# A fused network of attention, experts and gated taps: the sum of 16 weighted rows moves to GpSimd and TensorE, constants load in order of need, and each engine gets a new order

## What is computed

```python
x = _layernorm(x + _L0_attn_ref(x, ...))   # 16 heads of 8, softmax(q k' / sqrt(8) - slope * |i - j|) v, projection
x = _layernorm(x + _L0_ffn_ref(x, ...))    # top 2 of 8 experts silu(x W1 + b1) * (x W3 + b3) W2 + b2, and a shared one
x = _layernorm(x + _L1_attn_ref(x, ...))   # the block that the change touches, below
x = _layernorm(x + _L1_ffn_ref(x, ...))    # top 2 of 8 linear experts

# _L1_attn_ref, offsets 2^j * tau, of which 16 distinct ones are under 256
attn = softmax(stack([sum(q * shift(k, off)) * scale for off in OFFSETS]) + pos_bias)
out = sum(attn[off] * shift(v, off) for off in OFFSETS if off < N)
return (out * sigmoid(x @ w_gate + b_gate)) @ w_out + b_out
```

## Time and profile before

| | |
|---|---|
| runs | 1625.95 us median of 3 (1625.87 to 1630.54) |
| profiled execution | 1623.99 us, span 1622.2 us |
| busy share of the span | PE 87%, PEld 67%, DVE 84%, ACT 56%, POOL 46% |
| chain that ended last | DVE 39%, PE 39%, issue 10%, ACT 6%, DMA 2%, POOL 2%, SP 1% |
| TensorE clock granted, mean | 0.969 of 2.4 GHz |
| DMA | mean 111 GB/s |

### The profile page before, as it was taken

The page is one execution under the profiler, slowest core; times in us unless marked ns, Lnnn a source line. Parts: engine busy times, 40 slices in busy tenths (PEclk is TensorE's granted clock), DMA queues, the critical chain, the costliest instruction groups (busy, mean ns, idle before and its releaser), DMA issues.

```text
span 1622.2 us, 34112 instructions
## 1 busy us (share of the span) xinstructions
...
## 2 busy tenths in 40 slices
...
GB/s 170 91 86 131 121 107 101 128 134 123 95 127 134 100 101 128 135 124 92 128 132 102 101 127 133 105 107 134 113 102 114 134 122 88 119 92 87 77 45 39
DMA packets 83560, 179.69 MB, mean 111 GB/s; under 512 B 9771, under 2 KB 65835, under 8 KB 66219
## 3 DMA queue, kind: packets, MB, share of 16 engines
...
## 4 chain that ended last, share of the span: by engine, by line
DVE 39%; PE 39%; issue 10%; ACT 6%; DMA 2%; POOL 2%; SPq 1%; DVEq 0%; ACTq 0%; POOLq 0%
PE bPV L518 8%; DVE mneg L998 7%; DVE nDy L938 5%; PE bTU L547 4%; PE b L556 4%; DVE wb L900 4%; PE bTU L548 4%; DVE wb L961 3%; DVE gc L862 3%; ACT x L727 3%; PE bS L535 3%; PE b L421 2%; PE bTU L465 2%; DVE gat L979 2%; PE bTU L480 2%
## 5 line engine op out<-in xcount | busy, mean ns | idle before, releaser
L998 DVE TENSOR_REDUCE mneg<-bS 128x2 bf16<-128x512 f32 x512 | 342.2, 685 | 68.1 <-PE bS L538 68.1
L1058 POOL TENSOR_TENSOR wb<-wb 128x1024 f32<-128x1024 f32 x64 | 150.4, 2350 | 524.2 <-DVE wb L900 524.2
L1066 POOL TENSOR_TENSOR prod<-kC,qC 128x512 f32<-128x512 f32 x256 | 367.4, 1470 | 17.5 <-ACT kC L658 17.3
L696 ACT ACTIVATE sil<-bTU,b 128x256 f32<-128x256 f32 x288 | 133.2, 474 | 327.4 <-PE bTU L548 227.7
L686 ACT ACTIVATE P<-bTU 128x512 f32<-128x512 f32 x512 | 280.3, 597 | 32.9 <-PE bTU L482 32.3
L1078 POOL TENSOR_TENSOR h<-ub,gBcb 128x256 f32<-128x256 f32 x256 | 182.8, 727 | 248.9 <-DVE ub L1011 214.5
L535 PE MATMUL bS<-stack 96*128 96x256 bf16 x1024 | 225.7, 279 | 32.0 <-DVE mneg L998 25.8
L480 PE MATMUL bTU<-stack 97*128 97x256 bf16 x1024 | 214.0, 277 | 17.3 <-ACT P L686 15.3
L538 PE MATMUL bS<-dist,identh 128*128 128x128 f16 x1024 | 200.7, 223 | 0.0
L482 PE MATMUL bTU<-dist,identh 128*128 128x128 f16 x1024 | 194.2, 221 | 0.0
L547 PE MATMUL bTU<-x1T,w 128*128 128x256 f32 x576 | 181.0, 396 | 2.0 <-DVE ub L1011 2.0
...
## 6 DMA issues: line engine op xcount, KB each, us to landing
...
```

The costliest lines, as they stand in the source:

```text
L998: v.tensor_reduce(mneg[:, :, k], bS[k % 2][:].rearrange("p (a b) -> p a b", a=TT), op=ALU.max, axis=AX.X, negate=True).then_inc(dveS.done( ...
L1066: tt_(prod[:, 2 * p:2 * p + 2, :], shifted(kC, p), qC[:].unsqueeze(1).to_broadcast([128, 2, T]), ALU.mult).then_inc(poolC1.done("prod", p), 1)
```

## The change

- The first of VectorE's three additions becomes a third addition on GpSimd (`C2.add.2`, rows 0 to 3 plus rows 8 to 11), in its queue behind `C1.prod.1`.
- TensorE sums the remaining four rows with the identity as weights, four accumulating matmuls of 128x128 by 256 columns (`C2.sm`), into one of the three banks that are used in turn.
- `C2.gt` reads that bank instead of a row in SBUF. VectorE's three additions are gone.
- SyncE first loads only what pass 0 needs (xT and six DMAs, `ld_first`), then the score tables; the other 19 constant DMAs come behind `A1.rows.2` of pass 0. TensorE waits for them at the start of pass 1, and VectorE and ScalarE make the small tables (`tables()`) at the end of pass 1.
- All five queues get a new order.

```diff
 ORDER = {
     "pe": """
-        B2.z A1.qk S.s.0 A1.v A2.ST.0 A2.ST.1 S.s.1 S.s.2 A2.ST.2 A2.ST.3 A2.ST.4 S.s.3 S.s.4 A2.ST.5 A2.ST.6
-        A2.PV.0 B.xT A2.ST.7 S.s.5 D.xT A2.ST.8 B.lg C1.xT D.lg S.s.6 A2.ST.9 A2.ST.10 A2.PV.1 A2.ST.11 C1.qk
-        A2.ST.12 A2.ST.13 S.s.7 S.s.8 A2.ST.14 A2.ST.15 D.y.0 C1.vg B.cT A2.PV.2 S.s.9 D.y.1 B.ab.0 A2.PV.3 B.ab.1
-        S.s.10 B.ab.2 S.s.11 D.y.2 A3.pT S.s.12 B.ab.3 B.ab.4 S.s.13 C2.out B.ab.5 S.s.14 C1.sc A3.aT C1.scT B.ab.6
-        B.ab.7 B.ab.8 S.s.15 B.z C1.wT A3.out D.y.3 M.mT""",
+        A1.qk S.s.0 S.s.1 B2.z A2.ST.0 A1.v S.s.2 A2.ST.1 A2.ST.2 S.s.3 A2.ST.3 A2.ST.4 A2.ST.5 S.s.4 A2.ST.6
+        A2.PV.0 B.xT A2.ST.7 S.s.5 C1.xT S.s.6 D.xT A2.ST.8 A2.ST.9 B.lg S.s.7 D.lg A2.ST.10 A2.ST.11 A2.PV.1
+        A2.ST.12 A2.ST.13 C1.qk S.s.8 A2.ST.14 A2.ST.15 S.s.9 C1.vg D.y.0 A2.PV.2 D.y.1 B.cT B.ab.0 S.s.10 B.ab.1
+        S.s.11 S.s.12 A2.PV.3 S.s.13 C2.sm B.ab.2 A3.pT S.s.14 B.ab.3 B.ab.4 C2.out B.ab.5 S.s.15 C1.sc A3.aT B.ab.6
+        C1.scT B.ab.7 B.z D.y.2 D.y.3 A3.out C1.wT B.ab.8 M.mT""",
     "act": """
-        A1.qk A2.exp.0 A2.exp.1 A2.exp.2 A2.exp.3 C2n.nm A2.exp.4 A3n.nm A2.exp.5 B.xT D.xT B2.nm A2.exp.6 A2.exp.7
-        A2.exp.8 A2.exp.9 C1.xT D2.nm A2.exp.10 A2.exp.11 G.ge A2.exp.12 C1.qk A2.exp.13 A2.exp.14 B.cT A2.exp.15
-        B.ab.0 B.ab.1 A3.cp B.ab.2 B.ab.3 C1.vg B.ab.4 B.ab.5 C1.sc B.ab.6 A3.aT C1.exp B.ab.7 B.ab.8 C1.wT M.mT""",
+        A1.qk A2.exp.0 A2.exp.1 A2.exp.2 A2.exp.3 A2.exp.4 C2n.nm A3n.nm B2.nm A2.exp.5 A2.exp.6 B.xT C1.xT D.xT
+        D2.nm A2.exp.7 A2.exp.8 A2.exp.9 A2.exp.10 A2.exp.11 A2.exp.12 G.ge C1.qk A2.exp.13 A2.exp.14 A2.exp.15 B.cT
+        B.ab.0 B.ab.1 A3.cp C1.vg B.ab.2 B.ab.3 B.ab.4 C1.sc B.ab.5 A3.aT B.ab.6 C1.exp B.ab.7 C1.wT B.ab.8 M.mT""",
     "dve": """
-        B2.res D2.mom N.root.0 S.max.0 A1.rest N.root.1 S.max.1 S.max.2 N.root.2 A1.v N.root.3 S.max.3 A1.mid A1.lo
-        C2.pv.0 C2.pv.1 C2.pv.2 C2.pv.3 S.max.4 S.max.5 S.max.6 G.rank C2.pv.4 C2.pv.5 C2.pv.6 C2.pv.7 G.weigh
-        S.max.7 S.max.8 C2.add.0 D.acc.0 C2.add.1 D.acc.1 S.max.9 B.wu.0 B.wu.1 C2.add.2 S.max.10 C2.gt B.wu.2
-        D.acc.2 S.max.11 A3.rec S.max.12 C2.res A3.num S.max.13 B.wu.3 B.wu.4 B.wu.5 C1.mx S.max.14 S.max.15 B.wu.6
-        C1.sum B.wu.7 B.wu.8 A3.res D.acc.3""",
+        S.max.0 S.max.1 A1.rest B2.res D2.mom A1.v N.root.0 S.max.2 N.root.1 N.root.2 A1.mid N.root.3 S.max.3
+        S.max.4 A1.lo C2.pv.0 C2.pv.1 C2.pv.2 C2.pv.3 S.max.5 S.max.6 S.max.7 G.rank C2.pv.4 C2.pv.5 C2.pv.6 C2.pv.7
+        G.weigh D.acc.0 S.max.8 D.acc.1 S.max.9 S.max.10 S.max.11 B.wu.0 B.wu.1 S.max.12 C2.gt B.wu.2 S.max.13
+        A3.rec A3.num S.max.14 C2.res B.wu.3 S.max.15 B.wu.4 C1.mx B.wu.5 B.wu.6 C1.sum B.wu.7 A3.res D.acc.2 B.wu.8
+        D.acc.3""",
     "pool": """
-        C2.add.0 C2.add.1 C1.prod.0 C1.prod.1 C1.prod.2 C1.prod.3 C1.prod.4 C1.prod.5 C1.prod.6 C1.prod.7 B.h.1
-        B.h.2 B.h.3 B.h.4 B.h.5 A3.xbo B.h.6 B.h.7 C2.xb B.h.8""",
+        C2.add.0 C2.add.1 C1.prod.0 C1.prod.1 C2.add.2 C1.prod.2 C1.prod.3 C1.prod.4 C1.prod.5 C1.prod.6 C1.prod.7
+        B.h.1 B.h.2 B.h.3 B.h.4 A3.xbo B.h.5 B.h.6 C2.xb B.h.7 B.h.8""",
     "sp": """
-        C2.wb A1.part.0 A1.part.1 X.xT A3.x A1.part.2 B.cT A1.rows.0 B.cb A1.rows.1 A1.rows.2 D2.out C1.dw M.m C1.wb""",
+        C2.wb D2.out A1.part.0 A3.x A1.part.1 A1.part.2 B.cT X.xT B.cb A1.rows.0 A1.rows.1 A1.rows.2 C1.dw M.m C1.wb""",
 }
...
-        turn = [(what[-2:], n) for what, n in ORDER["pe"] if what in ("A2.ST", "B.ab", "D.y")]
+        turn = [(what[-2:], n) for what, n in ORDER["pe"] if what in ("A2.ST", "B.ab", "D.y", "C2.sm")]
...
-        consts = [(wqk0, "wqk0"), (bqk0, "bqk0"), (qs0, "qs0"), (wv0, "wv0"), (wo0, "wo0"), (gw0, "gw0"), (gw1, "gw1"),
+        first_consts = [(wqk0, "wqk0"), (bqk0, "bqk0"), (qs0, "qs0"), (wv0, "wv0")]
+        consts = [(wo0, "wo0"), (gw0, "gw0"), (gw1, "gw1"),
                   (b1, "b1"), (b3, "b3"), (b2, "b2"), (wc, "wc"), (bc, "bc"), (woc, "woc"), (ident, "ident"),
                   (hsum, "hsum"), (least, "least"), (posd, "posd"), (oobd, "oobd")]
         score_consts = [(identh, "identh"), (dist, "dist")]
         expert_consts = [(w13, "w13"), (w2, "w2"), (ew, "ew")]
...
-        N_CONST, N_SCORE, N_EXPERT = len(consts) + 1 + 3 * TT, len(score_consts) + 9, len(expert_consts)
+        N_CONST, N_SCORE, N_EXPERT = len(consts) + 1 + 2 * TT, len(score_consts) + 9, len(expert_consts)
+
+        N_FIRST = len(first_consts) + TT
...
-            for dst, name in consts:
-                sp.dma_start(dst[:], A[name]).then_inc(ld_const, 16)
-            sp.dma_start(identb[:].bitcast(U16), A["identb"]).then_inc(ld_const, 16)
+            for dst, name in first_consts:
+                sp.dma_start(dst[:], A[name]).then_inc(ld_first, 16)
             for tt in range(TT):
-                for dst, name in ((bv0, "bv0"), (bo0, "bo0"), (boc, "boc")):
-                    sp.dma_start(dst[:, tt, :], bass.AP(A[name].tensor, 0, [[0, 128], [1, 128]])).then_inc(ld_const, 16)
+                sp.dma_start(bv0[:, tt, :], bass.AP(A["bv0"].tensor, 0, [[0, 128], [1, 128]])).then_inc(ld_first, 16)
...
+                    if t == 0 and (what, n) == ("A1.rows", 2):
+                        for dst, name in consts:
+                            sp.dma_start(dst[:], A[name]).then_inc(ld_const, 16)
+                        sp.dma_start(identb[:].bitcast(U16), A["identb"]).then_inc(ld_const, 16)
+                        for tt in range(TT):
+                            for dst, name in ((bo0, "bo0"), (boc, "boc")):
+                                sp.dma_start(dst[:, tt, :],
+                                             bass.AP(A[name].tensor, 0, [[0, 128], [1, 128]])).then_inc(ld_const, 16)
...
-            pe.wait_ge(ld_const, 16 * N_CONST)
-            pe.wait_ge(setup_dve, SETUP_DVE)
-            pe.wait_ge(setup_act, SETUP_ACT)
+            pe.wait_ge(ld_first, 16 * N_FIRST)
...
+                if t == 1:
+                    pe.wait_ge(ld_const, 16 * N_CONST)
+                    pe.wait_ge(setup_dve, 12)
+                if t == LAG["C1"]:
+                    pe.wait_ge(setup_dve, SETUP_DVE)
+                    pe.wait_ge(setup_act, SETUP_ACT)
...
+                    if what == "C2.sm" and (e := r["C2"]) is not None:
+                        take(turn_bank("sm", 0), ("C2", dveC2, "gt", 0), t)
+                        o = bTU[turn_bank("sm", 0)]
+                        pe.wait_ge(poolSum.sem, poolSum.count(e, "add", 2))
+                        for x in range(4):
+                            i = mm(o[:, 0:T], ident[:], pv[:, x, :], start=(x == 0), stop=(x == 3))
+                        i.then_inc(peC2.done("sm"), 1)
...
+            act.wait_ge(setup_act, 1)
+
+            def tables():
+
+                act.wait_ge(ld_const, 16 * N_CONST)
+                nc.scalar.mul(bc[:, 0:1], bc[:, 0:1], q_scale).then_inc(setup_act, 1)
...
+                act.wait_ge(setup_dve, SETUP_DVE)
...
+            dve.wait_ge(ld_first, 16 * N_FIRST)
+            dve.wait_ge(setup_dve, 12)
+
+            def tables():
+
+                dve.wait_ge(ld_const, 16 * N_CONST)
...
-                    if what == "C2.add" and n == 0 and (e := r["C2"]) is not None:
-
-                        dve.wait_ge(poolC2.sem, poolC2.count(e, "add", 1))
-                        v.tensor_tensor(pv[:, 0:4, :], pv[:, 0:4, :], pv[:, 8:12, :], ALU.add).then_inc(dveC2.done("add", 0), 1)
...
-                    if what == "C2.add" and n == 1 and (e := r["C2"]) is not None:
-                        dve.wait_ge(dveC2.sem, dveC2.count(e, "add", 0))
-                        v.tensor_tensor(pv[:, 0:2, :], pv[:, 0:2, :], pv[:, 2:4, :], ALU.add).then_inc(dveC2.done("add", 1), 1)
...
-                    if what == "C2.add" and n == 2 and (e := r["C2"]) is not None:
-                        dve.wait_ge(dveC2.sem, dveC2.count(e, "add", 1))
-                        v.tensor_tensor(pv[:, 0, :], pv[:, 0, :], pv[:, 1, :], ALU.add).then_inc(dveC2.done("add", 2), 1)
                     if what == "C2.gt" and (e := r["C2"]) is not None:
 
-                        dve.wait_ge(dveC2.sem, dveC2.count(e, "add", 2))
+                        dve.wait_ge(peC2.sem, peC2.count(e, "sm"))
                         dve.wait_ge(actC1.sem, actC1.count(e, "g"))
                         dve.wait_ge(peC2.sem, peC2.count(e - 1, "out"))
-                        v.scalar_tensor_tensor(gat[:], tg[:], 1.0, pv[:, 0, :], ALU.add,
+                        v.scalar_tensor_tensor(gat[:], tg[:], 1.0, bTU[turn_bank("sm", 0)][:, 0:T], ALU.add,
                                                ALU.mult).then_inc(dveC2.done("gt"), 1)
...
 
-                        pool.wait_ge(dveC2.sem, dveC2.count(e, "pv", 4 * n + 3))
-                        tt_(pv[:, 8 * n:8 * n + 4, :], pv[:, 8 * n:8 * n + 4, :], pv[:, 8 * n + 4:8 * n + 8, :],
-                            ALU.add).then_inc(poolC2.done("add", n), 1)
+                        if n < 2:
```

(10 more changed lines are left out.)

60 lines of the change are left out of this document (30 added, 30 removed).

## The result

The changed kernel takes 1618.42 us, median of 5 runs (1615.07 to 1621.27), against 1625.95 for the kernel before; the ratio is 0.9938, with a 95% interval of 0.9914 to 0.9961. It is faster by 0.6%, where 1635 and "slower" were forecast; the range, 1606 to 1655, holds it. The profiled execution took 1620.27 us, its span 1618.5, 3.7 less than the span before.

A forecast was written before the change was run, and what follows sets the result against it. No engine is full; a dependence loop of three legs closing once per pass bounds the kernel. Profiled 1624.0 + 5 (steady passes) + 6 (last passes) - 1.5 (start) = 1633.5, plus 2.0 for the median: 1635; range 1606 to 1655.

The forecast's parts named there:

- Leg A: Stretch from the end of `C2.pv.7` to the start of `C1.sc`: GpSimd's queue would bound it, 16.3 us against 15.85.
- lower bound, 15.9: Bound on Leg A, if a second copy of an addition started behind a product loses no more than 1.9 us.
- TensorE's 15.2: When TensorE would be through its Leg A queue, in us after `pv.7`, 1.1 us before GpSimd's last product.
- the first rival: GpSimd is faster than its rows, so TensorE would end Leg A: pass 45.4 us, about 1606 in all; chance 0.15.
- Leg B: Stretch from the start of `C1.sc` to the start of `A3.res`, TensorE's: 9.9 us, taken as 10.0, against 10.60.
- Leg C: VectorE's stretch from the start of `A3.res` to the end of `pv.7`: 20.2 us, bounds 20.0 to 20.6, against 19.89.
- `G.rank` did not wait for `D.lg`: Sign in Leg C: `D.lg` returns at about 16.1 us, `G.rank` wants it at 16.3; a wait would refute the forecast.
- before `B.wu.3`, for the whole GpSimd queue: Expected sign: VectorE idle before `B.wu.3`, which needs `B.h.1` and hence all of GpSimd's queue.
- The pass: Steady pass, the sum of its three legs: 46.5 us against 46.3, bounds 45.8 to 47.2; +5 us over 25 full passes.
- The start: New loading order of constants: first matmul at about 7 us, `S.s.0` of pass 1 at 33.2; -1.5 us (-4 to +1).
- The last passes: Passes t = 32 to 36: additions among GpSimd's products and cold matmuls cost about +6 us (+2 to +9).
- rival 3: TensorE's clock falls more often because of longer idle around `A2.PV.0`: 8 more passes make 26 us, 1661; chance 0.2.

The follow-up runs named there:

- before_no_adds: The kernel before without VectorE's three additions and nothing in their place, so the gate reads an incomplete sum: 1607.62 us, ratio 0.9869.
- dummy_two: The changed kernel with an extra VectorE addition of 128x960, two SBUF inputs, on scratch ahead of `C2.gt`: 1616.56 us, one execution.
- dummy_one: The changed kernel with an extra VectorE maximum over 128x960, one SBUF input, ahead of `C2.gt`: 1616.01 us, one execution.
- no_consts: The changed kernel with the old loading: all constants first, tables before pass 0, all waits at the start: 1622.68 us, ratio 0.9952 to the kernel before.
- sm_one: The changed kernel with one of the four `C2.sm` matmuls, leaving three quarters of that sum out: 1600.10 us, ratio 0.9827 to the kernel before.

## Why the prediction was wrong

**Leg A is the step that failed.** The term was "0.08 + 2.31 + 11.57 + 2.31 + 0.06 = 16.3". The additional 2.31 is right (2.35 and 2.31 in the rows after). The 11.57 is not: it measured 2.33 + 7.35, 9.6 in the queue. It was the duration of the eight products in company of VectorE's additions, which the change removes. before_no_adds takes the additions out and changes nothing else, and the eight products take 9.82. The prediction priced this contention for VectorE alone (the first addition, 1.2 at its shortest and 2.2 in place) and never for the other partner, and its lower bound, 15.9, let no product get shorter. The trace before had the warning: products of 1176, 1278 and 2219 ns as shortest, median and longest, beside a mean of 1470. With the median the term would have been at most 10.2 and the end on GpSimd 0.08 + 2.31 + 10.2 + 2.31 = 14.9, below TensorE's 15.2; 14.32 was measured.

The prediction quoted the Trainium skill's GPSIMD Engine Reference, section "Specifications", that GpSimd's way to SBUF is shared with VectorE instructions of two SBUF inputs. dummy_two and dummy_one agree with the rule, at 0.9 us and 0 for an operation of 1.32 and 1.15 us. The prediction drew only one side from it, what VectorE loses. The other section that it named of the Trainium skill's GPSIMD Engine Reference, "Engine selection", speaks against the move. It holds for the single operation (2.35 on GpSimd against 1.21), and it decided nothing here, as GpSimd's queue had room.

**TensorE ends leg A**, as the first rival said, and its 15.2 was near: 15.62, with `C2.sm` starting at 8.67 instead of 8.4. The rival's reason was another one, though ("GpSimd is faster than its rows"), and its chance of 0.15 too small. Its time of 1606 was too low, mainly because leg A is 0.4 longer than its 15.2, leg C 0.4 longer than 20.2, leg B 0.2 shorter: 45.99 and not 45.4.

**Leg B** was 9.80 for 9.9 worked out and 10.0 taken. **Leg C** was 20.56 for 20.2, inside its bounds; line 864, the former 832, took 0.41 and met no addition, and `G.rank` did not wait for `D.lg`. 0.22 of the rest is a wait of `S.max` for scores; what makes the other 0.14 I didn't resolve. The gate took 0.42 at 10.65 after `pv.7` (forecast 0.47 at 10.4). `B.wu.2` came at 12.43 (12.2), but the waits named "before `B.wu.3`, for the whole GpSimd queue" didn't come: it was ScalarE that `B.wu.2` waited for.

**The pass**: 45.99 where 46.5 stood. 25 x 0.5 = 12.5 us is nearly all of the 13.2 us by which the forecast for the profiled execution, 1633.5, missed 1620.3; the lower bound of 45.8 held the value. The other 3.9 us between the medians are chance: the median before lay 2.0 above its profiled execution, the median after 1.9 below.

**The start**: the first matmul came at 8.03 (7 forecast), the last constants arrive and pass 1 starts at 33.37 (31 forecast), and its `S.s.0` at 35.24, so 0.5 us is gained on the 35.70 of the earlier trace rows and not 2.5. By pass 7 the lead is 3.24 us, and not 1.5, but it isn't the loading's: with the old loading (no_consts) it is 2.94. 2.3 us of it come between passes 4 and 7, which are filling passes and already gain by the new order. So the -1.5 for the loading is neither confirmed nor refuted: kernels with the same start reach pass 7 between 231.4 and 234.0, and its 0.15 to 0.25% of the whole time lie within the errors. **The last passes** gave back 8.7 instead of 6: the last two sums, at the lower clock, take 3.77 us each in the trace. In the drain VectorE's additions were worth 6.4 (before_no_adds) and three of the four matmuls 8.0 (sm_one), with the scatter told above.

**The clock**, rival 3, was half right. The new order does leave TensorE idle 0.78 and 1.60 us around `A2.PV.0` (1.2 and 1.5 forecast), and matmuls put there kept the clock up. But this execution had one long pass in place of two, so the falls added nothing to the time. A fall costs 4.5 us here against 3.3 in the earlier trace rows, as it lasts 10.2 us and not 6.8.

In sum, against the profiled 1624.0: the steady passes' +5 was -9.2 (including the clock), the stretch to pass 7 was -3.2 for the start's -1.5, the end's +6 was +8.7. That gives 1620.3, the profiled time.
